# Packed columns in the forward transform, another order of the turns, layer 0 in the loop

## What is computed

```python
x = transpose(coords @ fc0_w + fc0_b)                     # (64, 32, 64, 64)
for sw, cw, cb in layers:                                 # four
    x_ft = rfft2(x, norm='ortho')[:, :, :20, :20]         # 20 x 20 modes kept
    out  = einsum('bixy,ioxy->boxy', x_ft, sw)
    x1   = irfft2(out padded with zeros, s=(64, 64))
    x2   = einsum('bchw,oc->bohw', x, cw) + cb
    x = gelu(x1 + x2)
h = gelu(x @ fc1_w + fc1_b) @ fc2_w + fc2_b               # (64, 64, 64)
h = h + attention(layernorm(h)); h = h + experts(layernorm(h))
```

## Time and profile before

| | us |
|---|---|
| median of the timed runs | 1593.86 |
| profiled execution | 1591.21 |
| its span, first to last instruction | 1589.4 |
| TensorE matmuls busy | 1372.1 |
| VectorE busy | 1177.5 |
| ScalarE busy | 532.5 |
| turn_inverse, all | 304.7 |
| turn_w, all | 235.2 |
| dft_w matmuls, all | 206.8 |

### The profile page before, as it was taken

One profiled execution on the slowest core, in us unless ns is written; L12 is line 12 of the kernel. 1 busy time (PEld: TensorE's weight loads), 2 busy tenths in 40 slices (PEclk: granted clock), 3 DMA queues, 4 the chain that ended last, 5 costly groups with the idle time before them and its releaser, 6 DMA issues. The chain is left out here.

```text
span 1589.4 us, 69028 instructions
## 1 busy us (share of the span) xinstructions
PE 1372.1 (86%) x32216; PEld 702.5 (44%) x32216; DVE 1177.5 (74%) x1433; ACT 532.5 (34%) x673; POOL 92.4 (6%) x45
## 2 busy tenths in 40 slices
PE   9888888888888888878888888778879999989997
PEld 3444444445444444454444444555541115863332
DVE  3499999987899999878999998555540014978886
ACT  2422222222222222132222222343339996430221
POOL 1000000000000000000000000000000000017551
PEclk9999999999999999999999999999999999999998
DMA  6324233236655665566565664499998681037430
GB/s 223 111 110 161 109 147 123 109 147 220 243 233 225 238 238 219 205 214 243 231 234 222 236 238 173 183 372 378 378 373 325 251 295 59 8 91 170 117 81 14
DMA packets 59934, 315.80 MB, mean 199 GB/s; under 512 B 16704, under 2 KB 18688, under 8 KB 25984
## 3 DMA queue, kind: packets, MB, share of 16 engines
q1 hardware_dynamic: 36512, 177.95, 32.9%
q10 hardware_dynamic: 23264, 135.49, 20.8%
HBM read 176.05 MB, written 137.36 MB: 197 GB/s over the span
## 5 line engine op out<-in xcount | busy, mean ns | idle before, releaser
L889 ACT ACTIVATE act_c<-slots,conv_b 128x1024 f32<-128x1024 f32 x256 | 282.0, 1114 | 763.4 <-PE slots L579 763.4
L776 DVE STREAM_TRANSPOSE inv_out<-slots 128x1024 f32<-128x1024 f32 x256 | 304.7, 1229 | 152.3 <-PE slots L541 152.3
L579 PEld LDWEIGHTS slots<-inv_w,inv_out 64*64 64x64 f32 x16384 | 269.5, 135 | 197.7 <-issue 187.5
L579 PE MATMUL slots<-inv_w,inv_out 64*64 64x64 f32 x16384 | 300.3, 223 | 13.1 <-issue 7.5
L541 PE MATMUL slots<-turned_k,inv_h 64*64 64x320 f32 x2048 | 169.2, 444 | 102.6 <-DVE turned_h L752 75.1
L752 DVE STREAM_TRANSPOSE turned_h<-slots 128x1024 f32<-128x1024 f32 x200 | 235.2, 1218 | 26.2 <-PE slots L474 26.1
L474 PE MATMUL slots<-turned_w,fwd_w 32*64 32x512 f32 x3200 | 206.8, 609 | 37.4 <-DVE inv_out L776 33.3
L741 DVE STREAM_TRANSPOSE turned_w<-act_c 128x1024 f32<-128x1024 f32 x192 | 224.2, 1210 | 0.5 <-ACTq L892 0.5
L541 PEld LDWEIGHTS slots<-turned_k,inv_h 64*64 64x64 f32 x2048 | 69.1, 133 | 183.1 <-DVE turned_h L752 123.3
L486 PE MATMUL slots<-turned_h,fwd_h 64*64 64x320 f32 x1600 | 132.7, 443 | 1.3 <-DVE turned_h L752 1.3
L563 PE MATMUL slots<-xin,conv_w 32*32 32x512 f32 x3072 | 113.5, 612 | 22.5 <-DMA xin<-act_scratch 18.5
(11 more groups left out here) (166 smaller groups left out, 1114.8 us busy)
## 6 DMA issues: line engine op xcount, KB each, us to landing
act_scratch<-act_c ACTq DMA_DIRECT2D x128, 1024.0 KB, 4.0
xin<-act_scratch SPq DMA_DIRECT2D x96, 1024.0 KB, 4.8
act_c<-act_scratch SPq DMA_DIRECT2D x32, 1024.0 KB, 6.3
mode_w<-in_sw_dram SPq DMA_DIRECT2D x20, 640.0 KB, 4.8
at_turned<-level_scratch SPq DMA_DIRECT2D x24, 256.0 KB, 4.1
at_ret_t<-level_scratch SPq DMA_DIRECT2D x20, 256.0 KB, 4.1
xin<-in_x_dram SPq DMA_DIRECT2D x4, 1024.0 KB, 7.9
turned_w<-in_x_turned_dram SPq DMA_DIRECT2D x3, 1024.0 KB, 4.9
```

What stands on the lines that cost most here:

```text
L579: mm = nc.tensor.matmul(banks[half * 64:(half + 1) * 64, 2 * two + odd, at:at + 64], inv_out[rows, t % 2, i, two, s, 2 * half:2 * half + 2 ...
L776: nc.vector.transpose(dst, src).then_inc(inv_turned, 1)
L889: nc.scalar.activation(act_c[:, t % RING, :, at, :].rearrange("p i q m -> p q i m"), banks[:, at, :].rearrange("p q (i m) -> p q i m", i=2 ...
```

## The change

dft_w for pairs 1 to 27 of each forward layer computes the 20 kept modes as 16 + 4. The 16 low modes, real and imaginary, fill 32 rows; the 4 high modes of four groups of channels (SETS = 4) fill another 32. Low results take 1024 columns in banks 4 and 5, high ones 256 in banks 6 and 7, so turn_w turns 1280 columns, in two transposes. dft_h gets constants for this layout and 12 matmuls: for the real and the imaginary half each two of 320 columns, two of 192 and two of 128. turn_modes is issued between turn_w and turn_h, and for pair j+3. Layer 0 uses the same hardware loop; its coordinates come by four small DMAs per pair into the first 4 of each 32 rows, and first_w is one 32-column tile. (The function packed(n) says which pairs use the packed form.)

```diff
+LOW = 16
+HIGH = MODES - LOW
+SETS = 32 // (2 * HIGH)
+LOOPED = 4
...
+        def packed(n):
+            return n >= QUARTERS and 1 <= (n - QUARTERS) % PAIRS < PAIRS - LOOPED
...
+            def load_x(t):
+                if t >= IN_RING:
+                    sp.wait_ge(summed, after_out(0, t - IN_RING, 0))
+                for p in range(4):
+                    sp.dma_start(flat(xin[p * CH:p * CH + IN_CH, t % IN_RING]), x[t, p]).then_inc(
+                        xin_in[t % IN_RING], 16)
...
+            def packed_dft_w(n):
+                for wh in range(2):
+                    for step in range(SETS):
+                        if step % 2 == 0:
+                            at = slice(step * 128, step * 128 + 256)
+                            for i in range(2):
+                                for p in range(4):
+                                    q, rows_p = 2 * i + p % 2, slice(p * 32, (p + 1) * 32)
+                                    nc.tensor.matmul(banks[q * 32:(q + 1) * 32, 4 + p // 2, at], low_w[rows_p, wh, :],
+                                                     turned_w[rows_p, n % 2, wh, i, at], start=(wh == 0 and step == 0),
+                                                     stop=(wh == 1), skip_group_check=True)
+                        for i in range(2):
+                            for p in range(4):
+                                q, rows_p = 2 * i + 1 - p % 2, slice(p * 32, (p + 1) * 32)
+                                mm = nc.tensor.matmul(
+                                    banks[q * 32:(q + 1) * 32, 6 + p // 2, 0:128], high_w[rows_p, wh, step, :],
+                                    turned_w[rows_p, n % 2, wh, i, :].rearrange(
+                                        "p (m g c s) -> p g c m s", g=SETS, c=CH // SETS, s=2)[:, step],
...
+            def packed_dft_h(n, parity, at=0):
+                for ri in range(2):
...
...
-                        w = first_w[rows_p, t % LIFT_E, :] if l == 0 else conv_w[rows_p, l, :]
+                        w = first_w[rows_p, :] if l == 0 else conv_w[rows_p, l, :]
...
-                looped = 2 * ((PAIRS - 1 - first) // 2) if l > 0 else 0
+                looped = 2 * ((PAIRS - 1 - first) // 2)
...
             def turn_w(n):
                 dve.wait_ge(w_done, n + 1)
+                if packed(n):
+                    dve.wait_ge(h_done, n - 1)
+                    nc.vector.transpose(low_of(n).rearrange("p (b c m) -> p c b m", c=CH, m=2),
+                                        flat(banks[:, 4:6, :]).rearrange("p (n c s) -> p c n s", c=CH, s=2)).then_inc(
+                                            w_turned, 1)
+                    nc.vector.transpose(high_of(n).rearrange("p (k g c) -> p c g k", g=SETS, c=CH // SETS),
+                                        banks[:, 6:8, 0:128].rearrange("p b (c m) -> p c b m", m=16)).then_inc(
+                                            w_turned, 1)
+                    return
...
+                turn_modes(l, 2)
                 for j in range(PAIRS):
                     if j + 1 < PAIRS:
                         turn_inverse(l, j + 1)
-                    if j + 2 < PAIRS:
-                        turn_modes(l, j + 2)
+                    if not last and j >= 1:
+                        turn_act(l + 1, j - 1)
+                    if not last and j >= 2:
+                        turn_w(forward(l + 1, j - 2))
+                    if j + 3 < PAIRS:
+                        turn_modes(l, j + 3)
                     if last:
                         continue
```

More of the change, by code:

```diff
@@ L412, in _ @@
                 load_mode_w(0, pair)
[L413 to L414 removed]
+            for t in range(IN_RING):
+                load_x(t)
             for l in range(LAYERS):
@@ L465, in warm_up @@
                     nc.tensor.matmul(banks[:, 1, 384:512], w2_at[:, 0:128], w2_at[:, 0:128], start=True, stop=True)
+            def packed_dft_w(n):
+                for wh in range(2):
+                    for step in range(SETS):
[14 more added lines that the diff above has]
+                                        "p (m g c s) -> p g c m s", g=SETS, c=CH // SETS, s=2)[:, step],
+                                    start=(wh == 0 and step == 0), stop=(wh == 1 and step == SETS - 1),
+                                    skip_group_check=True)
+                mm.then_inc(w_done, 1)
@@ new lines, in packed_dft_h @@
+            def packed_dft_h(n, parity, at=0):
+                for ri in range(2):
+                    if ri == 0:
+                        take(w_turned, after_w_turned(n, 0))
+                    for i in range(2):
+                        rows_i = slice(i * 64, (i + 1) * 64)
+                        for kwh in range(2):
+                            first = ri * 32 * LOW + kwh * 320
+                            count = 320 if kwh == 0 else 32 * (LOW - MIXES)
+                            nc.tensor.matmul(banks[kwh * 64:(kwh + 1) * 64, at + i, 0:count],
+                                             packed_h[rows_i, parity, 0, ri, :],
+                                             low_of(n)[rows_i, first:first + count].rearrange(
+                                                 "p (b c m) -> p b m c", c=CH, m=2),
+                                             start=(ri == 0), stop=(ri == 1 and kwh == 0), skip_group_check=True)
+                    if ri == 0:
+                        take(w_turned, after_w_turned(n, 1))
+                    for i in range(2):
+                        rows_i = slice(i * 64, (i + 1) * 64)
+                        mm = nc.tensor.matmul(banks[64:128, at + i, 192:320], packed_h[rows_i, parity, 1, ri, :],
+                                              high_of(n)[rows_i, ri * 128:(ri + 1) * 128],
+                                              start=False, stop=(ri == 1), skip_group_check=True)
+                mm.then_inc(h_done, 1)
@@ L629, in _ @@
             pe.wait_ge(fc0_cols_set, 1)
[L630 to L633, removed]
+            nc.tensor.matmul(banks[:, 3, 0:CH], fc0_cols, conv_w[0:CH, 0, :],
+                             start=True, stop=True).then_inc(first_w_filled, 1)
             warm_up(1)
@@ L660, in _ @@
                 inverse_w(l, 0, 1)
-                first = 1 if last else 4
-                looped = 2 * ((PAIRS - 1 - first) // 2) if l > 0 else 0
+                first = 1 if last else LOOPED
+                looped = 2 * ((PAIRS - 1 - first) // 2)
                 for j in range(1, first):
                     step(l, j)
-                if looped:
-                    steps(l, first, looped)
+                steps(l, first, looped)
                 for j in range(first + looped, PAIRS):
```

82 lines of the change are left out of this document (53 added, 29 removed).

## The result

The changed kernel is slower: 1678.81 us (median of 4 runs) against 1595.34 for the kernel before on the same chip, a ratio of the means of 1.0513, with its 95% interval [1.0475, 1.0551]. I had forecast 1550 and a range up to 1596. Its profiled span is 1678.4 us against 1589.4, 89.0 more.

A forecast was written before the change was run, and what follows sets the result against it. It took a ring of VectorE's work and inverse_h's turnaround to bound the 9.05 us step, TensorE afterwards at 8.54. Terms -42 - 1 - 3 + 2 = -44 us gave 1547 profiled, 1550 median; range 1518 to 1596, about 80%.

The forecast's parts named there:

- What bounds before, and the order on VectorE: Loop over pairs: VectorE's work but turn_h, plus 1.37 us, makes the 9.05 us step; moving turn_modes removes 0.73 us.
- The ring: Cycle that sets the loop's step: all of VectorE's work but turn_h, then 1.37 us from inverse_h's start to turn_inverse's.
- Packed columns on VectorE: turn_w turns 1024 + 256 columns, not 2 x 1024; the 256 cost about 0.33 us, 0.80 us less.
- What is late next: Loop step after the change: TensorE, no longer VectorE, ends last; its path sums to 7.94 us before additions.
- The TensorE ring: Loop step walked with VectorE out of the way, from turn_inverse through dft_w, inverse_w, dft_h and inverse_h: 7.94 us.
- dft_w packed: dft_w's 16 matmuls become 96: 2.15 us to inverse_w's start instead of 1.90, bounds 1.96 and 3.15.
- pass rate: Slower rival, in dft_w: passes limited at 16.4 ns apiece, dft_w 3.15, step 9.54, 1631 us; 7%.
- The back edge: Loop's end, once in two steps: TensorE's semaphore instructions and branch delay inverse_h by 0.6 us, +0.30 per step.
- The code: Instruction fetch: layer 0's stream costs nothing today; leaving a loop +1, longer unrolled steps one more, +2 us in all.
- The rival's mechanism: Loop body no longer stays in TensorE's instruction memory, each back edge waits for a packet: step 9.32, 1613 us; 9%.
- Coordinates, lift weights, first steps: Small coordinate DMAs cost 0, mask and lift weights at the start -1, first steps about -1 in each of layers 0 to 2.
- small cover: Faster rival, in the loop: back edge overlaps and dft_w is at its lower bound, step 7.98, 1504 us; 12%.

The follow-up runs named there:

- split6: no_pack with each dft_w matmul of 512 columns cut into six of 84 or 86, still on eight 32x64 tiles: 1675.81 us.
- sixteen3: no_pack with dft_w of pairs 1 to 27 on sixteen 32x32 tiles, three matmuls of 170 or 172 columns per tile and half of w: 1676.48 us.
- no_pack: The changed kernel with packed() always false, keeping the new order, layer 0's loop and coordinates per pair: 1539.77 us, ratio 0.9640.
- order_only: The kernel before with turn_modes(j+3) issued between turn_w and turn_h and nothing else changed: 1550.83 us, ratio 0.9707.
- early_back: no_pack with seven of the back edge's nine semaphore instructions issued right behind a round's second dft_w: 1529.33 us, ratio 0.9598.
- high_only: The changed kernel with the 32 low matmuls of dft_w left out: 1570.51 us.
- flat_high: The changed kernel with dft_w's high matmuls reading 128 adjacent columns instead of pieces of two elements: 1679.84 us.
- early_packed: The changed kernel with seven of the back edge's nine semaphore instructions issued right behind a round's second dft_w: 1669.54 us, ratio 1.0482.

## Why the prediction was wrong, point by point

- *What bounds before, and the order on VectorE*: right. The ring was real; taking turn_modes out of it gave a step of 8.41 where VectorE's own sum had said 8.35.
- *Packed columns on VectorE*: right. turn_w's transpose of 256 columns is followed by its neighbour after 582.82 - 582.37 = 0.45, where I had 0.33. VectorE has slack for it.
- *What is late next*: right in form. The TensorE ring of 7.94 with 1.46 added is 9.40; measured 9.36 to 9.38.
- *dft_w packed*: this step failed. I took 2.15 with an upper bound of 3.15 and measured 3.36, which alone is +1.21 a step. I had dismissed a price per pass because the conv loads 32 weights in 0.25 us. I now read that row as a burst: its 0.49 us of waiting for VectorE just before left time for the instructions to queue up (an argument; no run isolates it). The rate at which a stretch of 96 matmuls runs is another number, and neither mix, whose 40 passes use four large groups, nor the conv shows it. The upper bound came from 64x64 tiles. What the runs put in its place: 12.7 ns per float32 matmul on sixteen tiles, 6.3 on eight, and 0.28 for the packed form's lengths and order. The rival "pass rate", with its 3.15 and 1631 us, was the nearest. By the rule of the Trainium skill ("Runtime: NRT & Kernel Launch", Instruction fetch mechanics) this dft_w would take 6.4 us; 384 instructions in 3.36 us are 8.8 ns each, so its size is contradicted. That more instructions for the same columns take longer, the runs do show.
- *The back edge*: right in kind, mis-sized. +0.86 in two steps, where I had +0.60: 9.36 and 10.22.
- *The code*: this term failed too. The rival's mechanism, a wait for code at each back edge, is absent, yet code cost 35 us, which I had at +2. After's body stays on the chip once it is there; getting it there is the price. Pairs 4 to 7 take 8.6, 17.5 and 8.7 us more than three steady steps, and in layer 1 up to 5 of the 17.5 are the lower clock. split6 and sixteen3 show the same with no packing, no_pack nothing, so it goes with the number of matmuls in the body and not with the packed form. I had taken to say that a stream of code costs nothing. It cost nothing where a step of 112 matmuls took 9.05 us and VectorE ended last; order_only's layer 0 shows it at 8.41 already. The count was wrong as well: 80 and 164 matmuls a step should have been 112 and 196, and 7.4 packets 6.1.
- *Coordinates, lift weights, first steps*: within 2 us each (-2.8 before the first turn_inverse, -2.9 in pairs 0 to 4). Layer 0 in the loop neither gained nor lost: 256.0 us in order_only and in no_pack.

One error needed no experiment. My own numbers gave the order edit alone a step of 8.35 (VectorE's sum, above a TensorE ring of 7.94 + 0.30), and the whole change 8.54. By them packing was a loss of 0.2 a step already. I never priced the parts against each other. (The rival "small cover" has 7.98 a step; its own terms, 7.94 + 0.06, give 8.00.) Even at my lower bound for dft_w, 1.96, the step is 8.0 with the edge hidden, 0.4 below early_back's 8.41: 81 x 0.4 = 33 us, about what the code costs at the loops' entries (estimates from the rows above).

What stays open is the mechanism inside TensorE. Neither one price per pass (high_only has 64 matmuls in 1.97), nor strides (flat_high), nor unevenness alone (sixteen3) gives all values; that two groups of tiles take 1.97 and 1.89 us alone and 3.36 together is measured, not explained. Of layer 1's entry the lower clock accounts for a part; early_packed shows the same (45.7 us at 0.85 there, 37.5 and 36.6 at 1.00 in layers 0 and 2). Why the clock falls in that entry is open, and so is the rest of its length.

## What to carry to other kernels

Price each part of a change alone against the ring that it leaves behind: once the order edit had removed 0.65 us, VectorE and TensorE were within 0.4 of each other, and a saving on one that adds instructions to the other had nothing to win. Take the cost of many small matmuls from a stretch as long as the new one, with the same tiles, and never from a burst that follows a wait. Count the instructions of a loop's body: they are paid once per entry of the loop, and beyond some size in every round.

## What the hardware showed that I had not expected

- A loop body of 2 x 196 float32 matmuls stays on the chip; 4 x 112 with the waits of four steps, or 2 x 228, is fetched again in each round, 8.8 packets of 16 KB. For 4 x 112 that made 1661.5 of 1539.8 us, 122 us in all for the same work, with a granted clock of 0.87 in the loop.
- Streaming a dense body in for the first time (2 x 196 matmuls, layer 1) stops TensorE for up to 4 us at a time, a packet coming every 3.4 to 6.2 us. In that layer the granted clock fell as well, to a mean of 0.89, and in layers 0 and 2 it stayed at 1.00.
- The same columns on sixteen 32x32 tiles instead of eight 32x64 took 2.27 against 1.91 us, before any cut.
- Semaphore instructions are free behind an unpacked dft_w (8.65 to 8.41) and show behind a packed one (0.60 us gap).
